# Scales and shifts of three norms folded into factors made ahead on GpSimd, in a linear-attention layer

## What is computed

```python
xn  = ln(x)
xc  = silu(conv(xn))                      # 4 taps over time
q, k, v = xn @ Wq.T, xn @ Wk.T, xn @ Wv.T
k   = l2(k); q = l2(q)
v   = ln(v) * vn_g + vn_b
dec = sigmoid(xc @ gamma_w.T + gamma_b)
kv  = k * v * sigmoid(xc @ ig_w.T + ig_b)
mem = scan(dec, kv)                       # m[t] = dec[t] * m[t-1] + kv[t]
o   = (ln(mem) * mn_g + mn_b) * q
o   = (ln(o) * gn_g + gn_b) * sigmoid(xc @ og_w.T + og_b)
x   = x + o @ Wo.T + (silu(xn @ w1.T) * (xn @ w2.T)) @ w3.T
```

## Time and profile before

| | us |
|---|---|
| median of 3 runs | 849.26 (848.54 to 850.39) |
| profiled execution, its own time | 849.49 |
| its span, first to last instruction | 847.5 |
| TensorE matmul busy | 742.0 (88%) |
| VectorE busy | 633.5 (75%) |
| ScalarE busy | 468.4 (55%) |
| GpSimd busy | 423.2 (50%) |

### The profile page before, as it was taken

How to read it: one execution, slowest core, us unless ns; L and a number is a source line. 1 busy time by engine, 2 the same in 40 slices (tenths; PEclk the granted TensorE clock), 3 DMA queues, 4 the chain that set the end, 5 groups by cost and what they waited for, 6 DMA issues and landing times. The chain is left out here.

```text
span 847.5 us, 15157 instructions
## 1 busy us (share of the span) xinstructions
PE 742.0 (88%) x5602; PEld 638.1 (75%) x5602; DVE 633.5 (75%) x1099; ACT 468.4 (55%) x746; POOL 423.2 (50%) x369
## 2 busy tenths in 40 slices
PE   3368799999999999999999999999779797988773
PEld 2256678888888888888888888888567686877662
DVE  6999877788777686777778777674373998988966
ACT  4246645755655664665566565567656454664411
POOL 2344454354355667658535435436436373763831
PEclk9579999999999999999999999999889999999985
DMA  5111121111011010110100000021100000000000
GB/s 157 28 39 39 39 77 46 45 40 45 3 33 40 21 52 21 39 46 20 28 21 3 21 3 20 21 77 40 52 1 0 1 1 26 1 26 1 1 26 25
DMA packets 22108, 25.89 MB, mean 31 GB/s; under 512 B 4498, under 2 KB 17170, under 8 KB 22036
## 3 DMA queue, kind: packets, MB, share of 16 engines
q1 hardware_dynamic: 22036, 24.93, 10.4%
HBM read 14.83 MB, written 3.28 MB: 21 GB/s over the span
## 5 line engine op out<-in xcount | busy, mean ns | idle before, releaser
L652 DVE TENSOR_REDUCE neg_max<-s_pair 128x4 f32<-128x1024 f32 x127 | 155.0, 1221 | 75.5 <-PE s_pair L866 75.3
L474 ACT ACTIVATE probs<-t_pair 128x1024 f32<-128x1024 f32 x128 | 131.3, 1025 | 135.9 <-PE t_pair L891 135.6
L371 POOL TENSOR_TENSOR hid<-g,hid 128x512 f32<-128x512 f32 x64 | 82.1, 1283 | 177.7 <-DVE g L763 144.6
L365 POOL TENSOR_TENSOR hid_lo<-hid,hid_hi 128x512 fp32r<-128x512 f32 x64 | 85.5, 1336 | 82.7 <-ACT hid_hi L497 82.6
L866 PE MATMUL s_pair<-K,Q 96*128 96x256 f32 x508 | 84.8, 290 | 16.1 <-DVE neg_max L652 9.8
L866 PEld LDWEIGHTS s_pair<-K,Q 96*128 96x128 f32 x508 | 75.5, 194 | 24.5 <-issue 8.1
L891 PE MATMUL t_pair<-Q,K 104*128 104x512 f32 x256 | 85.6, 416 | 0.3 <-DMA Q<-max_parts 0.3
L933 PE MATMUL down<-hi,hid_hi 128*128 128x256 f32 x256 | 83.9, 328 | 0.8 <-POOL hid_lo L365 0.8
L906 PE MATMUL misc<-probs,V 128*32 128x256 f32 x1024 | 69.4, 389 | 4.0 <-DVE kc L608 2.5
L933 PE MATMUL down<-lo,hid_hi 128*128 128x256 f32 x256 | 71.5, 279 | 0.0
L933 PE MATMUL down<-hi,hid_lo 128*128 128x256 f32 x256 | 71.2, 278 | 0.0
(11 more groups left out here) (258 smaller groups left out, 1962.9 us busy)
## 6 DMA issues: line engine op xcount, KB each, us to landing
stage<-in_ternary SPq DMA_DIRECT2D x18, 256.0 KB, 2.8
Q<-q_hi SPq DMA_DIRECT2D x64, 64.0 KB, 2.0
stage<-in_scales SPq DMA_DIRECT2D x8, 384.0 KB, 3.3
X<-in_x SPq DMA_DIRECT2D x8, 256.0 KB, 4.4
Q<-q_lo SPq DMA_DIRECT2D x32, 64.0 KB, 2.0
Q<-max_parts SPq DMA_DIRECT2D x128, 4.0 KB
out<-X SPq DMA_DIRECT2D x8, 256.0 KB, 2.3
signs<-w_stage SPq DMA_DIRECT2D x9, 128.0 KB, 1.8
```

The lines of the kernel that those rows point to most:

```text
L365: pool.tensor_tensor(hid_lo[:, m % 2, :, :].rearrange("p a n -> p (a n)"), hid[:, m % 2, :], hid_hi[:, m % 2, :, :].rearrange("p a n -> p ...
L371: pool.tensor_tensor(hid[:, m % 2, :], g[:, m % 2, :], hid[:, m % 2, :], ALU.mult).then_inc(S["hid_done"], 1)
L474: act.activation(probs[:, u % 2, th, :], t_pair[:], ACT.Exp, scale=SCALE).then_inc(S["probs_done"], 1)
L652: dve.tensor_reduce(neg_max[:, u % 2, 4 * jp:4 * jp + 4], score_banks(u, jp)[:].rearrange("p (s n) -> p s n", n=SEQ), AX_X, ALU.max, negat ...
```

## The change

Three norms end in "times scale, plus shift, times a factor": values (factor: keys), memory (factor: queries), output (factor: output gate). Before, each ran as linked steps after the norm, one pair on VectorE and one on GpSimd. Now GpSimd makes two products of the factor ahead, factor times shift and factor times scale; VectorE multiplies the raw data by the second in its PSUM bank, applies the norm's root to that product in the bank, and adds the first. Both pairs run this way on VectorE. For the values, the keys' root and the values' root are multiplied into one (`both`), and GpSimd scales the shift part by the keys' root (`keys_normed`). `hidden_low`, `through_input_gate` and `mlp_added` change places in the written orders, `queries_kept` moves behind `output_high`, and `gamma(m)`, `ffn_down(b)` wait for other semaphores.

```diff
-        def values(engine, early, b):
...
-        def memory_scaled(engine, late, b):
...
-        def gated(engine, late, b):
...
# GpSimd
+                def keys_weighted(b):
+                    wait = waiter(pool, early)
+                    k = qk[:, 1, pair(b), :]
+                    wait("qk_copied", 2 * b + 2)
+                    wait("b_turned", 0)
...
+                    inc(pool.tensor_tensor(heads(vn[:, pair(b), :]), heads(k), vn_b, ALU.mult), "kw_done")
+                    wait("kw_done", 2 * b + 1)
+                    inc(pool.tensor_tensor(heads(k), heads(k), vn_g, ALU.mult), "kw_done")
+                def keys_normed(b):
+                    wait("norm_done", 1)
+                    wait("kw_done", 2 * b + 2)
+                    inc(pool.tensor_tensor(heads(vn[:, pair(b), :]), heads(vn[:, pair(b), :]), each(ss[:, b, PAIR_HEADS:2 * PAIR_HEADS]), ALU.mult), "kw_done")
+                def queries_weighted():
+                    wait("q_kept", 1)
+                    wait("o_turned", 0)
...
+                    for b in range(BPG):
+                        inc(pool.tensor_tensor(heads(o[:, pair(b), :]), heads(q_kept[:, pair(b), :]), mn_b, ALU.mult), "mq_done")
+                    for b in range(BPG):
+                        wait("mq_done", b + 1)
+                        inc(pool.tensor_tensor(heads(q_kept[:, pair(b), :]), heads(q_kept[:, pair(b), :]), mn_g, ALU.mult), "mq_done")
+                def gates_weighted():
+                    wait("mw_done", BPG)
+                    wait("gates_done", TPG)
+                    for b in range(BPG):
+                        inc(pool.tensor_tensor(q_kept[:, pair(b), :], gates[:, 1 + late % 2, pair(b), :], gn_b2, ALU.mult), "gw_done")
+                    for b in range(BPG):
+                        g = gates[:, 1 + late % 2, pair(b), :]
+                        wait("gw_done", b + 1)
+                        inc(pool.tensor_tensor(g, g, gn_g2, ALU.mult), "gw_done")
+                def output_weighted(b):
+                    wait("cen_sq", b + 1)
+                    wait("gw_done", BPG + b + 1)
+                    inc(pool.tensor_tensor(o[:, pair(b), :], o[:, pair(b), :], gates[:, 1 + late % 2, pair(b), :], ALU.mult), "xg_done")
                 if late is None:
                     xn_low(pool, early, 1)
                     scaled()
+                    keys_weighted(0)
                     convolved()
+                    keys_weighted(1)
                     output_weights()
                     hidden_low(pool, early, 1)
-                    values(pool, early, 0)
+                    keys_normed(0)
+                    keys_normed(1)
                     hidden_low(pool, early, 2)
...
-                memory_scaled(pool, late, 1)
+                queries_weighted()
                 if early is not None:
                     hidden_low(pool, early, 1)
+                    keys_weighted(0)
                     convolved()
                     hidden_low(pool, early, 2)
-                    values(pool, early, 0)
+                    keys_weighted(1)
+                gates_weighted()
+                if early is not None:
+                    keys_normed(0)
+                    keys_normed(1)
+                output_weighted(0)
+                if early is not None:
                     hidden_low(pool, early, 3)
+                output_weighted(1)
+                if early is not None:
                     hidden_low(pool, early, 4)
                     through_input_gate(pool, early, 0)
-                gated(pool, late, 0)
-                if early is not None:
                     hidden_low(pool, early, 5)
                     through_input_gate(pool, early, 1)
# ScalarE
                 if early is not None:
-                    queries_kept()
                     hidden_high(5)
                 for b in halves:
                     output_high(b)
+                if early is not None:
+                    queries_kept()
# VectorE, end of norms_summed
+                    for b in range(BPG):
+                        v = turned(banks[b][:])
+                        wait("kw_done", 2 * b + 2)
+                        inc(dve.tensor_tensor(v, v, qk[:, 1, pair(b), :], ALU.mult), "vw_done")
# VectorE, norms, behind the root
+                    both = ss[:, :, 2 * PAIR_HEADS:]
+                    link(dve.tensor_tensor(both, both, ss[:, :, PAIR_HEADS:2 * PAIR_HEADS], ALU.mult), early, 0)
+                    wait("vw_done", BPG)
...
-                        inc(dve.tensor_tensor(heads(v if b else vn[:, pair(b), :]), heads(v), each(ss[:, b, 2 * PAIR_HEADS:]), ALU.mult), "vn_done")
+                        inc(dve.tensor_tensor(heads(v), heads(v), each(both[:, b, :]), ALU.mult), "vn_done")
+                def values_added(b):
+                    wait("vn_done", b + 1)
+                    wait("kw_done", 5 + b)
+                    inc(dve.tensor_tensor(vn[:, pair(b), :], turned(banks[b][:]), vn[:, pair(b), :], ALU.add), f"kv_done{b}")
# VectorE, memory_summed, behind each sum
+                        wait("mq_done", BPG + b + 1)
+                        y = turned(banks[4 + b][:])
+                        inc(dve.tensor_tensor(y, y, q_kept[:, pair(b), :], ALU.mult), "mw_done")
# VectorE, memory_normed
+                    for b in range(BPG):
+                        wait("mn_done", b + 1)
+                        inc(dve.tensor_tensor(o[:, pair(b), :], turned(banks[4 + b][:]), o[:, pair(b), :], ALU.add), f"op_done{b}")
# VectorE, output_applied
+                    for b in halves:
+                        y = turned(banks[4 + b][:])
+                        wait("xg_done", b + 1)
                         inc(dve.tensor_tensor(heads(y), heads(o[:, pair(b), :]), each(s2[:, b, :]), ALU.mult), "on_done")
+                    for n, b in enumerate(halves):
+                        wait("on_done", n + 1)
+                        inc(dve.tensor_tensor(o[:, pair(b), :], turned(banks[4 + b][:]), q_kept[:, pair(b), :], ALU.add), f"o_done{b}")
# VectorE, order of turn 0
                     norms()
                     hidden(1)
+                    values_added(0)
+                    values_added(1)
                     hidden_low(dve, early, 0)
-                    values(dve, early, 1)
# VectorE, order of the other turns
                     hidden(1)
-                memory_scaled(dve, late, 0)
...
                     hidden(3)
-                    values(dve, early, 1)
                 output_centered(1)
+                if early is not None:
+                    values_added(0)
+                    values_added(1)
                 if early is not None:
                     hidden(4)
                     mlp_added(0)
                     mlp_added(1)
                 output_summed()
-                if early is None:
-                    mlp_added(0)
-                    mlp_added(1)
                 output_normed()
...
                 output_applied()
-                gated(dve, late, 1)
                 if early is not None:
                     hidden(5)
+                else:
+                    mlp_added(0)
+                    mlp_added(1)
# TensorE
                 def ffn_down(b):
-                        if b == 0:
-                            wait("op_done0", 1)
-                        wait("mn_done", b + 1)
+                        wait(f"op_done{b}", 1)
                 def gamma(m):
                     wait("xc_lo_done", KC)
-                    if m == 0:
-                        wait("vn_done", 1)
-                    else:
-                        wait("kv_done1", 1)
+                    wait(f"kv_done{m}", 1)
```

More of the change, by code:

```diff
@@ L1140, in hidden_low @@
             inc(engine.tensor_tensor(h_lo[:, at, :], hid[:, c % 2, :], h_hi[:, at, :].bitcast(F32), ALU.subtract), f"h_lo_done{c}")
-        def values(engine, early, b):
-            wait = waiter(engine, early)
-            wait("vn_done", b + 1)
-            wait("qk_copied", 2 * b + 2)
-            v, k = turned(banks[1][:]) if b else vn[:, pair(b), :], qk[:, 1, pair(b), :]
-            inc(linked(engine, wait, f"kv_link{b}", [
-                (heads(v), heads(v), vn_g, ALU.mult),
-                (heads(v), heads(v), vn_b, ALU.add),
-                (heads(k), heads(k), each(ss[:, b, PAIR_HEADS:2 * PAIR_HEADS]), ALU.mult),
-                (k, k, v, ALU.mult)]), f"kv_done{b}")
         def through_input_gate(engine, early, b):
@@ L1156, in through_input_gate @@
             wait(f"kv_done{b}", 1)
[L1157 to L1176 removed]
+            inc(engine.tensor_tensor(vn[:, pair(b), :], vn[:, pair(b), :], gates[:, 0, pair(b), :], ALU.mult), f"b_done{b}")
         @block.sync
@@ L1366, in queries_kept @@
                     wait("norm_done", 1)
-                    wait("op_done0", 0)
-                    wait("op_done1", 0)
+                    wait("o_done0", 0)
+                    wait("o_done1", 0)
                     wait("ro_done", 0)
```

43 lines of the change are left out of this document (17 added, 26 removed).

## The result

The changed kernel takes 910.38 us in the median of four runs (907.92 to 911.49); the kernel before took 849.54 beside it (848.54 to 850.39). The ratio is 1.0713, with an interval of 1.0686 to 1.0739: slower by 60.8 us, where 53.9 had been forecast (903 us, range 883 to 917). The profiled execution took 907.92 us, its span is 906.1.

A forecast was written before the change was run, and what follows sets the result against it. No engine idle to take work; the order of queue waits bounds the kernel. Turns 0 to 4: +7.9, +19.6, +19.9, +10.7, -4.2, together +53.9 on 849.5, less 0.2: 903 us, range 883 to 917.

The forecast's parts named there:

- The first wait: VectorE in `norms_summed` waits for GpSimd's `keys_weighted(1)`, queued behind `convolved` and `hidden_low(2)`: 8.7 us in each of turns 1 to 3.
- H: Start of the third `hidden` multiply on VectorE in a turn of the second layer; 726.85 us in the profile before.
- turn 2: Third of five second-layer turns (0 to 4), each starting with its scan: 69.7 us forecast against 49.8, +19.9.
- turn 0: First second-layer turn: VectorE's wait in `norms_summed` delays the third `hidden` multiply from 638.81 to 646.8, +7.9 us.
- The second wait: TensorE's `gamma(0)` waits for VectorE's `values_added(0)`, until H + 23.9 instead of H + 9.6, idling some 15 us.
- the slow clock at its start: TensorE at the 1.2 GHz level from `gamma`, after idling some 15 us: 1.8 us added, bounds 0 and 3.4.
- The lock: VectorE instructions with two SBUF inputs and GpSimd ones reading SBUF exclude each other: some 13 us of the total.
- Turn 4: Last turn: `mlp_added` leaves the chain, two VectorE additions replace GpSimd's `gated`, a slow output product takes 1 back: -4.2 us.
- Turn 3: No group ahead, so neither its 3.6 us on TensorE nor the taps: 63.4 us against 52.7, +10.7.
- the slow clock in the tail: Rival: TensorE's 1.2 GHz level returns, half of the tail's 13 us doubled, 6 us a turn: 920 to 925; chance 0.11.
- The rival that forecast a gain: GpSimd leaves the turn's end, neither VectorE nor `gamma(0)` waits (`values_added(0)` by H + 9.6): 841 us, chance 0.03.

The follow-up runs named there:

- The run with the keys first: From the changed kernel, GpSimd makes both halves' weighted keys ahead of `convolved`: 893.28 us, ratio 1.0527 to the kernel before.
- the run with the root in a bank: Output's scale and shift folded into the kernel before, products behind `hidden_low(2)`, first half's root written to a PSUM bank instead of SBUF: 848.14 us, 0.9991.
- the output's part alone: Four runs from the kernel before, folding only the output's scale and shift, the last only in the last turn: 850.72, 856.24, 848.14 and 848.45 us.
- the run with the output's shift apart: Only the output folded into the kernel before, shift products in the convolution sigmoid's buffer, products behind `hidden_low(2)`, `values(0)` after `hidden_low(3)`: 856.24 us, 1.0081.
- the first run of the output's part: Only the output's scale and shift folded into the kernel before, products ahead of `convolved` and in the queries' buffer: 850.72 us, 0.9988.

## Why the prediction was right, and where it was off

**The first wait: right.** Forecast: VectorE stands 8.7 us, until H + 13.3. Measured in turn 2: 8.32 us, until H + 12.9 (768.57 less 755.63). H itself came at the scan + 18.5 (forecast 18.3), and turn 0 shows the same wait with 7.14 us. The run with the keys first took it down to 0.70 us, so it is that order and nothing else.

**The second wait: right.** `gamma(0)` started at H + 23.2 (forecast 23.9), after 14.62 us of idle time (forecast some 15); `hidden(4)` at H + 29.4 (29.9), the output's turning at H + 41.9 (42.8), the next scan 7.8 us later (8.6). Every step of turn 2 came out within 1 us, the 1.8 us for the slow clock at its start among them (2.05 us against 1.16 for the first four matmuls, 2.85 against 1.98 for the eight of `ffn_up`). The chain had one link more than the text had weighed: behind the two waits stood a third, `keys_normed` behind `gates_weighted`, which added nothing in the middle turns and came up only when the first was gone.

**The lock: right in kind, not in each size.** In the tail of turn 2 the two taps took 2.76 us against 2.15 before, 0.6 more where the text had 2.0. The runs make the kind firmer than the earlier trace rows could. In the changed kernel's turn 4 four small instructions each waited for one of GpSimd's; in the run with the root in a bank, one operand moved took the wait away. The Trainium skill's page SBUF — State Buffer, section Who interferes with whom, has it as an exclusive lock held for a whole instruction, and the rows agree: a VectorE instruction ends about when GpSimd's does (1.29 to 1.19 us each beside four of 1.26), no matter how little it reads.

**Turn 4: wrong.** The term was -4.2 us and it came out +1.6. The step that failed is the one by which GpSimd's `gated` "is replaced by two additions on VectorE": it priced what leaves the end of the chain and did not look for the lock at its start, where `gates_weighted` begins just as the root begins. Those four instructions took 4.93 us instead of 0.88, which is 4.1 of the miss of 5.8 us; the run that moves `gates_weighted` behind the root shortened the turn by 3.1 us. Of the rest, 0.8 is one more small instruction that waited (888.98, 1.02 us for 0.23) and 1.0 the way from the last half of the output to the last residual, 7.5 us against 5.5, where the text had allowed 1 more: its 24 matmul records, 897.35 to 902.60, all ran at a granted clock of 0.50.

**Turn 3: too low by 1.9 us.** The tail was taken at 5.9 us and took 8.3, from the turning at 862.27 to the scan at 870.59. First the turning, then the busy time of the first 14 of the 24 output matmuls, which ran at a granted clock of 0.50:

```profile
862.27 1.25 PE L1881 MATMUL lbank<-ident,rows 128*128 128x128 f32 x8
```

```profile
865.33:868.40 3.07, 3.07 (x14) 3.07 (x15) 0.65 (x2) 0.81 (x2) 3.07 (x4) 0.50 0.00 0
```

The text gives no rows for its 5.9, and the kernel before contradicts it. From its chain that ended last, turn 3, the turning:

```profile
805.47 1.13 PE lbank L1834 x4
```

From there to the scan at 813.57 it was 8.1 us already, with slow output matmuls as well. So the change added next to nothing to this tail, and the term could have been read off. The text had the slow clock in the tail only in a rival, over half of the tail and in every turn; of turns 1 to 3 it came in one, in one step, and in turns 1 and 2 the output's matmuls ran at 1.00.

**The sum.** 58.6 us by the spans against 53.9. The two turns with both waits at their fullest came out 2.6 lower together, turns 0, 3 and 4 together 8.8 higher (5.8 of it turn 4), the first layer 1.4 lower. That the sum is within 5 us rests in part on these misses going both ways.

**The rival that forecast a gain** named its point: both waits must go. The runs show that this is not enough. With both gone, and the third, the kernel is still 13 us slower (`gamma(0)` no longer waits there because it stands later; `values_added(0)` itself starts at H + 15.5 in turn 2, not at the H + 9.6 that the rival asked for); the output's part alone was tried in four forms, and the best of them is level with the kernel before or a microsecond better. What GpSimd gives back at the end of a turn is lost again to its further instructions where VectorE has two SBUF inputs, to the two multiplies at the front, and to TensorE's clock. How much each takes was not separated, and whether an order exists that gains more was not settled.

## What to carry to other kernels

Before a step goes to an engine that works strictly in order, write down what stands in front of it there and who waits at its end: GpSimd, idle half of the time, had its products ready at H + 12.9 us, where VectorE wanted them at H + 4.6. Count GpSimd's instructions not by its idle time but by what VectorE runs beside them, operand by operand; a chain of small dependent instructions on SBUF paid a whole GpSimd instruction for every link here, and a link with one input in a bank did not. Undo such a change part by part rather than step by step: two waits in a row hide each other, and mending one shows less than it is worth.

## What the runs showed of the hardware that was not expected

- The wait for GpSimd also hits a small instruction with a single SBUF input: the `tensor_scalar` at 876.33, 64 columns, took 1.29 us beside GpSimd, the one at 876.11 just before GpSimd began 0.18.
- It goes both ways: GpSimd's instructions of 512 columns took 1.75 us beside the locked multiplies in the run with the output's shift apart and, in the changed kernel's turn 2, 1.26 to 1.27 while VectorE stood.
- TensorE's level after a gap was not the same each time. After 1.90 us of idle time the output's products of turn 1 ran at a granted clock of 1.00, after 1.81 us those of turn 2 at 0.50, both in the run with the output's shift apart; and the second `ffn_up` of turn 2, after 2.70 us of idle time, took 3.78 us in the first run of the output's part and 2.12 in the one with the root in a bank. So the idle time just before does not decide it; what does, was not tried.
